# Turning gh and half of z off TensorE, and the order of projections and products around it

## The reference, cut to what matters

```python
# x (32, 64, 1024) f32, ids (32,), W (1024, 1024), Wr (8, 1024), A (8, 16, 1024),
# B (8, 1024, 16), U (1024, 256), S (256,), V (1024, 256)
base = einsum('btd,od->bto', x, W)
logits = einsum('btd,ed->bte', x, Wr) + 5.0 * one_hot(ids)[:, None, :]
topw, topi = top_k(logits, 2)
gates = sum(one_hot(topi, 8) * softmax(topw)[..., None], axis=-2)
h = einsum('btd,erd->bter', x, A)
cond = base + 2.0 * einsum('bter,bte,eor->bto', h, gates, B)
out = x + einsum('bti,oi->bto', cond, (U * S) @ V.T)
```

## Time and profile before

| what | us |
|---|---|
| median of 3 runs (153.8 to 154.09) | 153.99 |
| the profiled execution's own time | 154.44 |
| its span, first to last instruction | 152.7 |
| TensorE busy in the span | 147.4 |
| VectorE busy | 107.2 |
| GpSimd busy | 72.3 |
| ScalarE busy | 63.5 |
| mean busy share of the 16 DMA engines over q1 | 55.8% |

### The profile page before, as it was taken

The page is one execution under the profiler, slowest core; times in us unless marked ns, Lnnn a source line. Parts: engine busy times, 40 slices in busy tenths (PEclk is TensorE's granted clock), DMA queues, the critical chain, the costliest instruction groups (busy, mean ns, idle before and its releaser), DMA issues.

```text
span 152.7 us, 2912 instructions
## 1 busy us (share of the span) xinstructions
PE 147.4 (97%) x1056; PEld 139.1 (91%) x1056; DVE 107.2 (70%) x297; ACT 63.5 (42%) x141; POOL 72.3 (47%) x57
## 2 busy tenths in 40 slices
PE   7799999999999999999999999999999999999991
PEld 5699999999999989998999899989999998998880
DVE  0488887759478999978765875587558736795851
ACT  4397876894546422446014612351334105013000
POOL 2000242993560659292966186636655640721700
PEclk9999999999999999999999999999999999999998
DMA  5999999999303030049719903980591068006184
GB/s 171 315 400 409 400 405 411 410 407 409 132 6 137 0 137 4 0 192 345 288 60 350 386 34 136 338 347 10 211 286 57 0 277 262 17 0 275 69 339 142
DMA packets 10670, 32.72 MB, mean 214 GB/s; under 512 B 1441, under 2 KB 1953, under 8 KB 10529
## 3 DMA queue, kind: packets, MB, share of 16 engines
q1 hardware_dynamic: 10368, 31.96, 55.8%
q10 hardware_dynamic: 288, 0.59, 1.2%
HBM read 24.16 MB, written 8.39 MB: 213 GB/s over the span
## 4 chain that ended last, share of the span: by engine, by line
PE 93%; DMA 3%; ACT 0%; DVE 0%; SPq 0%; issue 0%; DVEq 0%
PE fin L343 13%; PE fin L345 13%; PE fin L344 13%; PE pj L344 10%; PE pj L343 10%; PE pj L345 10%; PE zt L343 6%; PE zt L345 6%; PE zt L344 6%; DMA w_raw<-in_W 3%; PE gt L447 1%; PE zt L434 1%; PE fin L380 1%; PE gt L344 1%; PE gt L345 1%; PE fin L390 1%
## 5 line engine op out<-in xcount | busy, mean ns | idle before, releaser
L281 POOL TENSOR_TENSOR xT_lo<-xt_raw,xT_hi 128x1024 fp32r<-128x1024 f32 x15 | 36.5, 2443 | 25.2 <-DVE gh L801 7.9
L304 POOL TENSOR_TENSOR x_all<-x_all,vw_raw 128x512 f32<-128x512 f32 x21 | 26.6, 1297 | 25.8 <-DVE vw_raw L849 25.8
L343 PE MATMUL pj<-proj_hi,xT_hi 128*128 128x264 f32 x128 | 36.9, 288 | 0.0
L344 PE MATMUL pj<-proj_lo,xT_hi 128*128 128x264 f32 x128 | 36.3, 284 | 0.0
L345 PE MATMUL pj<-proj_hi,xT_lo 128*128 128x264 f32 x128 | 36.2, 283 | 0.0
L343 PE MATMUL fin<-v_hi,w_hi 128*128 128x256 f32 (+1 forms) x80 | 25.7, 321 | 0.0
L344 PE MATMUL fin<-v_lo,w_hi 128*128 128x256 f32 (+1 forms) x80 | 25.6, 320 | 0.0
L345 PE MATMUL fin<-v_hi,w_lo 128*128 128x256 f32 (+1 forms) x80 | 25.6, 320 | 0.0
L344 PEld LDWEIGHTS pj<-proj_lo,xT_hi 128*128 128x128 f32 x128 | 24.1, 189 | 0.2
L343 PEld LDWEIGHTS pj<-proj_hi,xT_hi 128*128 128x128 f32 x128 | 24.1, 188 | 0.2
L345 PEld LDWEIGHTS pj<-proj_hi,xT_lo 128*128 128x128 f32 x128 | 24.0, 188 | 0.0
(11 more groups left out here) (100 smaller groups left out, 282.5 us busy)
## 6 DMA issues: line engine op xcount, KB each, us to landing
xt_raw<-in_xt SPq DMA_DIRECT2D x16, 512.0 KB, 7.6
x_all<-in_x SPq DMA_DIRECT2D x16, 512.0 KB, 6.5
out<-x_all SPq DMA_DIRECT2D x13, 512.0 KB, 3.2
vw_raw<-in_VW SPq DMA_DIRECT2D x6, 384.0 KB, 7.1
w_raw<-in_W SPq DMA_DIRECT2D x8, 256.0 KB, 6.6
out<-x_all SPq DMA_DIRECT2D x5, 256.0 KB, 2.0
w_raw<-in_U SPq DMA_DIRECT2D x1, 1024.0 KB, 8.8
aw_raw<-in_AW SPq DMA_DIRECT2D x1, 544.0 KB, 7.2
```

Source lines behind the costliest of these rows:

```text
L281: nc.gpsimd.tensor_sub(xT_lo[:, t % XTR, :, :], xt_raw[:, t % XTR, :, :], xT_hi[:, t % XTR, :, :].bitcast(F32)).then_inc(xt_lo, 1)
L304: nc.gpsimd.tensor_add(x_all[:, t % XR, cols], x_all[:, t % XR, cols], ups[:, j, :]).then_inc(side_add, 1)
L343: nc.tensor.matmul(dst, l_hi, r_hi, start=first, stop=False, skip_group_check=shared)
L344: nc.tensor.matmul(dst, l_hi, r_lo, start=False, stop=False, skip_group_check=shared)
```

## The change

For pairs 1 to 6 TensorE turns neither gh nor z any more. VectorE turns the 32 x 32 blocks inside a tile with its own transpose (`turn_z` straight from PSUM, in the middle of the gates; `turn_gh` for both tiles) into `blk`; then twelve SBUF to SBUF transfers per pair, issued by SyncE, carry the off-diagonal blocks to their places in `tr`, and ScalarE copies the four diagonal ones (`move_diagonal`). Each transfer moves 32 partitions x 4 matrices x 32 elements, that is 128 pieces of 128 bytes. Pairs 0 and 7 are turned by TensorE as before.

The turned half of z is added to the LoRA part by VectorE, in a `sums` of five operations, four of which read both inputs from SBUF; the one-time split of the 7 blocks is done by `split_zb` alone. z^T gets two banks, `zt` and the one that held the turned gh.

The order changes on every engine. TensorE's step p is now project(2p), project(2p+1), half_t(p), first_part(p-2), mix(p-1), second_part(p-2); in step 2 mix(1) comes last, in step 7 mix(6) comes ahead of the products. ScalarE and GpSimd split x^T of tiles 2p+4 and 2p+5 in `pair(p)`, one step earlier than before; SyncE's loads stay where they were in its list, with the twelve moves between the loads and `store_pair`. GpSimd no longer waits for gh.

```diff
+            def move_blocks(p):
+                sp.wait_ge(blk_done, 3 * p)
+                for i in range(SQS):
+                    for j in range(SQS):
+                        if i != j:
+                            sp.dma_start(tr[SQ * j:SQ * (j + 1), p % 2, :, SQ * i:SQ * (i + 1)],
+                                         blk[SQ * i:SQ * (i + 1), p % 2, :, SQ * j:SQ * (j + 1)]).then_inc(tr_load, 16)
...
                 if 2 * p >= XR:
                     load_x(2 * p)
                     load_x(2 * p + 1)
+                if p < PAIRS - 1:
+                    move_blocks(p)
                 if p >= 2:
                     store_pair(p - 2)
...
             pool.wait_ge(us_lo_done, MC)
+            split_x(6)
+            split_x(7)
             for p in range(2, PAIRS):
-                if p < PAIRS - 1:
-                    split_x(2 * p + 2)
+                if p < PAIRS - 2:
+                    split_x(2 * p + 4)
                 sides(p - 2)
-                if p < PAIRS - 1:
-                    pool.wait_ge(gh_done, 2 * p + 2)
-                    split_x(2 * p + 3)
+                if p < PAIRS - 2:
+                    split_x(2 * p + 5)
             sides(PAIRS - 2)
...
             for p in range(1, PAIRS):
                 project(2 * p)
+                project(2 * p + 1)
+                zt_free(p)
+                half_t(p)
+                if p == PAIRS - 1:
+                    mix(p - 1)
                 if p >= 2:
                     first_part(p - 2)
-                project(2 * p + 1)
+                if 3 <= p < PAIRS - 1:
+                    mix(p - 1)
+                if p == PAIRS - 1:
+                    transpose_gh(p)
                 if p >= 2:
                     second_part(p - 2)
-                zt_free(p)
-                half_t(p)
-                transpose_gh(p)
+                if p == 2:
+                    mix(1)
...
             def pair(p):
-                if p < PAIRS - 1:
-                    split_x(2 * p + 2)
-                split_za(p - 1)
-                copy_x22(p - 1)
-                copy_u(p - 2)
-                copy_z(2 * p)
-                exp_top(2 * p)
-                split_zb(p - 1)
-                if p < PAIRS - 1:
-                    split_x(2 * p + 3)
-                copy_z(2 * p + 1)
-                exp_top(2 * p + 1)
-                split_gh(p)
+                exp_top(2 * p)
+                exp_top(2 * p + 1)
+                if p >= 3:
+                    split_gh_moved(p - 1)
+                if p < PAIRS - 2:
+                    split_x(2 * p + 4)
+                copy_u(p - 2)
+                if p == 2:
+                    split_gh_moved(1)
+                move_diagonal(p)
+                if p < PAIRS - 2:
+                    split_x(2 * p + 5)
+                copy_half(p - 1)
+                split_zb(p - 1)
...
+                nc.vector.tensor_add(zs[:, 0:8:7, :], zt_v[p % 2][:, 0, :, :], tr[:, p % 2, 2:4, :]).then_inc(z0_done, 1)
+                dve.wait_ge(z0_done, p)
+                nc.vector.tensor_add(zs[:, 3, :], zs[:, 7, :], zs[:, 2, :]).then_inc(sums_done, 1)
                 dve.wait_ge(sums_done, n + 1)
-                nc.vector.tensor_sub(zs[:, 2, :], zs[:, 1, :], zt_v[:, 0, 0, :]).then_inc(sums_done, 1)
+                nc.vector.tensor_sub(zs[:, 4, :], zs[:, 3, :], zs[:, 0, :]).then_inc(sums_done, 1)
                 dve.wait_ge(sums_done, n + 2)
-                nc.vector.tensor_sub(zs[:, 3, :], zs[:, 0, :], zs[:, 2, :]).then_inc(sums_done, 1)
-                nc.vector.tensor_sub(zs[:, 4, :], zt_v[:, 1, 0, :], zs[:, 2, :]).then_inc(sums_done, 1)
+                nc.vector.tensor_sub(zs[:, 5, :], zs[:, 2, :], zs[:, 4, :]).then_inc(sums_done, 1)
+                nc.vector.tensor_sub(zs[:, 6, :], zs[:, 1, :], zs[:, 4, :]).then_inc(sums_done, 1)
...
+            def gates(t):
+                gates_top(t)
+                if 2 <= t < TILES - 2:
+                    turn_z(t)
+                gates_apply(t)
+
             def pair_2():
                 split_zb(0)
                 split_us(1)
-                split_za(1)
+                gates(4)
+                gates(5)
+                turn_gh(2)
                 up(0, 1)
                 up(0, 2)
                 xb1(0)
-                sums(1)
-                gates_top(4)
-                gates_apply(4)
-                gates_top(5)
-                gates_apply(5)
+                split_gh_moved(1)
                 xa0(0)
                 xb0(0)
                 xa1(0)
-                split_gh(2)
+                sums(1)
...
             def pair(p):
-                split_zb(p - 2)
-                split_za(p - 1)
-                sums(p - 1)
-                gates_top(2 * p)
-                gates_apply(2 * p)
+                gates(2 * p)
+                if p == 3:
+                    split_zb(1)
+                gates(2 * p + 1)
+                turn_gh(p)
+                split_gh_moved(p - 1)
                 up(p - 2, 1)
                 up(p - 2, 2)
                 xb1(p - 2)
                 xa0(p - 2)
-                gates_top(2 * p + 1)
-                gates_apply(2 * p + 1)
+                sums(p - 1)
                 xb0(p - 2)
                 xa1(p - 2)
-                if p == PAIRS - 1:
-                    split_zb(p - 1)
-                split_gh(p)
+                split_zb(p - 1)
```

More of the change, by code:

```diff
@@ L420, in project @@
                                   proj_hi[:, k, 0:TCOLS], proj_lo[:, k, 0:TCOLS], k == 0, k == DC - 1)
-                    if t >= 2 and t % 2 == 0 and k == MH:
-                        mix(t // 2 - 1)
+                    if t == 2 and k == MH:
+                        mix(0)
                 last.then_inc(pj_done, 1)
@@ L430, in half_t @@
                                   xT_hi[:, r:r + 2, k, :], xT_lo[:, r:r + 2, k, :], k == 0, False, shared=True)
-                    if k == MH + 1:
-                        pe.wait_ge(z_copied, 2 * p + 2)
+                    if k == MH + 1 and (p == 0 or p == PAIRS - 1):
+                        pe.wait_ge(z_copied, 2 if p == 0 else 4)
                         for t in range(2):
-                            nc.tensor.matmul(zt_v[:, 0, t, :], z_sb[:, t, :], ident[:, :], start=False, stop=False,
+                            nc.tensor.matmul(zt_v[p % 2][:, 0, t, :], z_sb[:, t, :], ident[:, :], start=False, stop=False,
                                              is_transpose=True, skip_group_check=True)
@@ L653, in split_gh @@
             def split_gh(p):
-                act.wait_ge(gt_done, p + 1)
-                nc.scalar.copy(ghT_hi[:, :], gt_both).then_inc(gt_hi, 1)
+                act.wait_ge(gt_done, 1 if p == 0 else 2)
+                nc.scalar.copy(ghT_hi[:, :], (gt if p == 0 else pj[0])[:, 0:2 * P]).then_inc(gt_hi, 1)
             def copy_z(t):
@@ L721, in _ @@
             split_za(0)
-            copy_x22(0)
+            nc.scalar.copy(zs[:, 2, :], zt_v[0][:, 1, 1, :]).then_inc(zb_copied, 1)
             split_t(1)
-            copy_z(2)
+            split_x(5)
             exp_top(2)
             split_zb(0)
-            copy_z(3)
             exp_top(3)
-            split_x(5)
-            split_gh(1)
-            for p in range(2, PAIRS):
+            move_diagonal(1)
+            split_x(6)
+            split_x(7)
+            for p in range(2, PAIRS - 1):
                 pair(p)
+            last_pair(PAIRS - 1)
             copy_u(PAIRS - 2)
@@ L787, in gates_top, with turn_z, turn_gh @@
                                         ALU.is_equal).then_inc(gate_step, 1)
+            def turn_z(t):
+                nc.vector.transpose(blk[:, (t // 2) % 2, 2 + t % 2, :], pj[t % 2][:, Z0:TCOLS]).then_inc(blk_done, 1)
+            def turn_gh(p):
+                dve.wait_ge(gh_done, 2 * p + 2)
+                nc.vector.transpose(blk[:, p % 2, 0:2, :], gh[:, :, :]).then_inc(blk_done, 1)
             def gates_apply(s):
@@ L902, in pair, with last_pair @@
                 xa0(p - 2)
-                gates_top(2 * p + 1)
-                gates_apply(2 * p + 1)
+                sums(p - 1)
                 xb0(p - 2)
                 xa1(p - 2)
-                if p == PAIRS - 1:
-                    split_zb(p - 1)
+                split_zb(p - 1)
+            def last_pair(p):
+                gates(2 * p)
+                gates(2 * p + 1)
+                split_gh_moved(p - 1)
+                sums(p - 1)
+                up(p - 2, 1)
+                up(p - 2, 2)
+                xb1(p - 2)
+                xa0(p - 2)
+                split_zb(p - 1)
                 split_gh(p)
+                xb0(p - 2)
+                xa1(p - 2)
             dve.wait_ge(vw_load[0], 16)
@@ L939, in _ @@
             split_za(0)
-            sums(0)
-            gates_top(2)
-            gates_apply(2)
-            gates_top(3)
-            gates_apply(3)
+            sums_first()
+            gates(2)
+            gates(3)
+            turn_gh(1)
             split_t(1)
```

(4 more changed lines are left out.)

113 lines of the change are left out of this document (81 added, 32 removed).

## The result

The changed kernel takes 167.45 us (median of 4 runs, 166.83 to 168.39), the kernel before 153.9 on the same chip (153.35 to 154.09). The ratio is 1.088 with a 95% interval of 1.083 to 1.094: slower by 13.5 us. The profiled execution took 166.96 us, its span 165.2. TensorE's mean granted clock, of full speed, was 0.979 in it and in the one of 166.83, and 0.959 in the other two (167.95 and 168.39).

A forecast was written before the change was run, and what follows sets the result against it. TensorE, busy 97% of the span, bounds the kernel: 14.6 us of new waits less 2.6 gained is 12.0 over the profiled 154.44; timed runs lie 0.45 lower, giving 166.0 us. Likeliest case 159.3 to 169.5; eight in ten 152.0 to 169.5.

The forecast's parts named there:

- The gain: TensorE: six of eight pairs lose two pairs of transposes, 2.64 us, all that the change can win.
- The step of 14.14 us: TensorE's new length of a pair's step if nothing waits, against 14.58 us before.
- The port as turns: Shared VectorE/GpSimd port: a VectorE instruction reading two SBUF inputs costs one queued GpSimd instruction, 1.3 or 2.4 us.
- Rival 1: VectorE keeps the port through its chained sums, only one waits, steps 4 and 5 lose nothing: 156.5 us; chance 0.17.
- rival 2: Faster: the shared port is rarely met and all is covered, 151.35 to 152.8 us; chance 0.24.
- The loop through the store and x^T: Steps 4 and 5: late sums delay store, x^T load, copy_u and p2, reproducing the lateness; 4.0 us each.
- D: Time in a step at which the first store of the older pair goes out; 7.25 us forecast for steps 4 and 5.
- The threshold of 3.3: TensorE's p2 waits for copy_u when the store leaves more than 3.3 us into the step.
- Step 2: Waits at p2 (2.0 us), p4 (0.8) and mix(1) (0 to 0.7), together 2.8 to 3.5, taken as 3.0.
- The issues of the moves: SyncE: twelve issues a pair at 0.4 us each, 4.8 us, ending at 13.4 in the step, ahead of the stores.
- Rival 3: SyncE late: moves' issues take 12 us, 158 alone, over 169 with the port or clock falls; chance 0.09 including anything dearer.
- Steps 6 and 7: Late copy_u and p4 cost 1.7 us in step 6; mix(6) and p1(6) wait 1.6 us in step 7.

The follow-up runs named there:

- experiment 1: The kernel before with the 24 TensorE transposes of pairs 1 to 6 left out and nothing in their place: 151.54 us, ratio 0.986.
- experiment 7: The changed kernel with GpSimd's three side additions per pair cut from 512 to 8 columns each: 159.14 us, ratio 1.037.
- experiment 9: Experiment 8 with copy_u before the x^T split, GpSimd's splits behind gh and the sums, the moved gh's split ahead of the gates: 159.47 us, ratio 1.037.
- experiment 10: Experiment 9 with the split of the moved gh behind the gates again in pair 3, on both engines: 158.21 us, ratio 1.028.
- experiment 2: The changed kernel with SyncE loading x^T one step earlier: 160.12 us, ratio 1.039.
- experiment 3: The changed kernel with one of the twelve moves per pair kept and the other eleven left out: 164.0 us, ratio 1.070.
- experiment 6: The changed kernel with GpSimd doing the sides first and both x^T splits after the sums: 164.17 us, ratio 1.065.
- experiment 5: The changed kernel with copy_u ahead of the x^T split on ScalarE: 165.88 us, ratio 1.077.
- experiment 8: Experiment 2 with GpSimd's x^T splits of tiles 6 and 7 held until gh of tiles 4 and 5 is ready: 160.40 us, ratio 1.044.
- experiment 12: Experiment 11 with the split of the moved gh behind the gates in pair 4 too, on both engines: 159.11 us, ratio 1.033.
- experiment 11: Experiment 10 with GpSimd's step 3 splits of x^T tiles 8 and 9 waiting for gh of tiles 6 and 7, not the sums: 160.81 us, ratio 1.047.
- experiment 4: The changed kernel with one transfer of all of blk in place of the twelve moves, the diagonal copies waiting for it: 171.38 us, ratio 1.116.

## Why the prediction came out right

The forecast was 166.0 us, the result 167.45, and the mechanism was the one described. By its own steps:

- **The gain**, 2.64 us: measured 2.3, with an interval that holds 2.64 (experiment 1). The step of 14.14 us is confirmed: 14.16 to 14.19 where nothing waits (experiments 7, 9 and 10).
- **The port as turns.** Confirmed with the sizes given: 1.17 to 1.26 beside a side, 2.4 beside a split, gate instructions 2.07 and 2.18. Rival 1, that VectorE keeps the port through chained sums, is refuted by the sums of steps 4 and 5, and rival 2 by all of them. Experiment 7 adds that without the sides' length the loss of steps 4 and 5 all but goes, and experiment 2 that it also goes, but for 0.65 and 1.4, with an earlier load: it takes both, the long sums and the load behind the store.
- **The loop through the store and x^T.** D was put at 7.25 and measured 6.06 and 6.53. As worked out ahead, three of the four sums of 128 columns were long; ahead of step 5, where TensorE's end of the step came 0.1 us later than put (3.1 behind `copy_u`), VectorE's list from `copy_u` to xa1 took 9.6 us in place of 10.2. In step 4 the x^T landed later than put, 7.05 us after the store in place of 6.3, which gave part of the difference back. The steps were 3.6 and 3.1 us too long for 4.0 each. The threshold of 3.3 held to within the reading (experiment 7), and with x^T loaded early the 3.6 and 3.1 fell to 0.65 and 1.4 (experiment 2).
- **Step 2** is the term that was mis-sized: 3.0 forecast, 6.6 measured. The issues of the moves were taken at 0.4 us, inside bounds of 0.34 and 1, and took 0.65. I had asked only whether they delay the stores; in step 2 they stand ahead of the x^T load. That made the gap 4.1 in place of 2.2 us, and the clock fell, 2.7 us more; the waits forecast at p4 and mix(1), 0.8 and up to 0.7 us, were covered by the slow matmuls. Rival 3 had both in it, at a chance of 0.09, but at steps 4 and 5, where they did little. In its profile experiment 3 takes both away together, and the step of 17.8 us is then 0.7 over the forecast's 14.14 + 3.0 = 17.1. Rival 3's "with the port, over 169" adds two delays that run side by side: the store waits for whichever ends last. In the changed kernel the moves ahead of the store of 90.70 were issued by 87.81, in experiment 6 they were the later.
- **Steps 6 and 7**: 1.0 and 1.25 for 1.7 and 1.6.

The misses cancel: step 2 was put 3.6 too low and steps 3 to 7 2.45 too high. Another 0.6 us no term covers: in the profile after, project(0) starts at 28.20, in the one before at 28.82 and in the other profiles anywhere from 27.7 to 28.7, before any pair is done: a difference between executions, not between the kernels. That leaves the 0.5 us between the 166.44 that the sum gives for the profiled execution and its 166.96. So the mechanism was right and the closeness of the total is luck.

**What was wrong in the experiments' forecasts** is mostly one thing: experiments 5 and 8 to 12 took a wait away and counted the whole of it as won, and missed by 3 us and more. Two things stood behind the wait. In experiments 8, 10 and 12 it was GpSimd: its instruction is still there and meets VectorE's next one with two SBUF inputs, or holds back GpSimd's own sides. In 5, 9 and 11 it was the moves, which had not landed when the sums or the split of gh came to them.

**Open.** What makes the clock fall. In the profiles it fell at gaps of 4.14 us (changed kernel, step 2), 4.37 (experiment 6), 4.43 (experiment 7), 3.49 (experiment 4), 3.51 (experiment 9) and 3.81 (experiment 11), but also at 2.10 (experiments 2 and 10); it stayed up at 3.54 and 3.03 (changed kernel, steps 4 and 5) and 2.34, 2.61 and 2.98 (experiment 3). The length of the gap alone doesn't tell these apart. Nor is it fixed by the program: two of the changed kernel's four executions had a mean clock of 0.959 in place of 0.979, which is some 6.6 us more at half level (an estimate: 0.02 x 166 x 2), and took 1.0 to 1.6 us longer. The single profile of each experiment shows one such outcome.

## What to carry to other kernels

Work taken off the bounding engine is worth its own time and no more (here 2.3 us), so first count what it adds on the engines that release that engine's next work. When a consumer is moved a step earlier in a hand-ordered pipeline, move its load as well, and list what stands ahead of that load in its queue. While GpSimd has work queued, a VectorE instruction with two SBUF inputs can each time last until one GpSimd instruction is over (1.26 us beside a side, 2.4 beside a split, in place of 0.29): its price is GpSimd's instruction and not its own size, so many short ones in a chain are a dear form.

## What the hardware showed

- A move of 32 partitions x 4 x 32 elements within SBUF takes SyncE's queue 0.65 us to issue (12 in 7.81 us), a 512 KB store that isn't held up 0.34. The data of a move land 1.9 us after the issue. q1's share rises only from 55.8% to 56.2%, but of a longer span: from 85.2 to 92.8 us of all 16 engines, 7.6 us more for 1.2 MB. By these numbers, as an estimate, the pieces of 128 bytes moved at some 155 GB/s of engine time and the rest, 32.0 MB, at 375; that is 1.3 us a pair, spread over a step, and no wait of TensorE in the changed kernel names a move. What they cost there was the issues. The single transfer of 128 partitions (experiment 4) took the queue 0.47 to 0.53 us.
- VectorE's transpose takes 0.31 us for 128 x 128 float32 from PSUM and 0.45 us for 128 x 256 from SBUF, 1.07 a pair. The Trainium skill ("VectorE: DVE Perf Modes", The three transpose paths) gives 311 ns for 128 x 128 in bf16, and the 307 ns measured here in float32 are close to that:

```profile
L853 DVE STREAM_TRANSPOSE w_raw<-pj 128x128 f32<-128x128 f32 x12 | 3.7, 307 | 0.0
L857 DVE STREAM_TRANSPOSE w_raw<-gh 128x256 f32<-128x256 f32 x6 | 2.7, 446 | 0.2
```

- In the profiles the granted clock fell at a gap for 3.41 or 6.83 us at half level, and there were gaps of 3.54 us with no fall and of 2.10 us with one.
